# NF4 weights w1 and w2 quantised in the turned layout: block scales through memory in place of PE transposes

## What is computed

```
def nf4_quant_dequant(w):
    flat = w.reshape(-1, 64)
    absmax = max(abs(flat), axis=1, keepdims=True)
    normalized = flat / where(absmax == 0, 1.0, absmax)
    idx = searchsorted((NF4_CODE[:-1] + NF4_CODE[1:]) * 0.5, normalized)
    return (NF4_CODE[idx] * absmax).reshape(w.shape)
x = layernorm(x + layer1(x))
dq1, dq2, dq3 = (nf4_quant_dequant(w) for w in (w1, w2, w3))   # w1, w2: 1376 x 512, w3: 512 x 1376
h = silu(x @ dq1.T) * (x @ dq2.T)
out = layernorm(x + h @ dq3.T)
```

## Time and profile before

| | |
|---|---|
| median of 3 runs | 429.08 us (428.99 to 429.38) |
| the profiled execution | 429.23 us, its span 427.4 us |
| PE busy | 417.5 us, 98% |
| DVE, POOL, ACT busy | 307.1, 293.0, 265.2 us |
| PE transposes of w1 and w2 (L1258) | 88 instructions |
| moved by DMA | 26.51 MB |

### The profile page before, as it was taken

The page is one execution under the profiler, slowest core; times in us unless marked ns, Lnnn a source line. Parts: engine busy times, 40 slices in busy tenths (PEclk is TensorE's granted clock), DMA queues, the critical chain, the costliest instruction groups (busy, mean ns, idle before and its releaser), DMA issues.

```text
span 427.4 us, 5638 instructions
## 1 busy us (share of the span) xinstructions
PE 417.5 (98%) x1908; PEld 342.9 (80%) x1908; DVE 307.1 (72%) x379; ACT 265.2 (62%) x356; POOL 293.0 (69%) x230
## 2 busy tenths in 40 slices
PE   8999999999999999999999999999999999999992
PEld 6888888888878888888878888888888877888881
DVE  3639989979879966978358889978699974216025
ACT  5576776677668554638837797788677864332612
POOL 0079999888784698248943788899989993444330
PEclk9999999999999999999999999999999999999997
DMA  8994110000013442020060000000000000000202
GB/s 266 399 352 157 51 38 25 26 25 26 25 49 107 145 141 72 0 100 1 0 265 1 2 0 2 0 2 0 2 2 0 2 0 0 2 0 2 98 0 99
DMA packets 10876, 26.51 MB, mean 62 GB/s; under 512 B 1472, under 2 KB 1728, under 8 KB 10336
## 3 DMA queue, kind: packets, MB, share of 16 engines
q1 hardware_dynamic: 10848, 26.16, 17.8%
HBM read 24.06 MB, written 2.10 MB: 61 GB/s over the span
## 4 chain that ended last, share of the span: by engine, by line
PE 88%; ACT 3%; DVE 3%; issue 2%; POOL 2%; DMA 1%; SPq 0%; ACTq 0%; POOLq 0%
PE PS L1144 28%; PE PS L1145 28%; PE PS L1146 28%; PE PS L1258 2%; DMA h<-xT 1%; PE PS L1269 1%; ACT x_hi L557 1%; ACT l_hi L557 1%; POOL x_lo L1088 1%; POOL l_lo L1099 1%; DVE std L894 1%; DVE stats L875 0%; ACT R L643 0%; DVE R L870 0%; PE PS L1244 0%
## 5 line engine op out<-in xcount | busy, mean ns | idle before, releaser
L1069 POOL TENSOR_SCALAR level<-side 128x1024 f32<-128x1024 int8 (+2 forms) x119 | 133.0, 1118 | 13.7 <-ACT side L557 4.1
L1144 PE MATMUL PS<-x_hi,w_hi 128*128 128x512 f32 (+1 forms) x352 | 138.4, 393 | 0.3 <-DVE x_lo L944 0.3
L1146 PE MATMUL PS<-x_hi,w_lo 128*128 128x512 f32 (+1 forms) x352 | 137.2, 390 | 0.0
L1145 PE MATMUL PS<-x_lo,w_hi 128*128 128x512 f32 (+1 forms) x352 | 137.1, 390 | 0.0
L800 DVE TENSOR_TENSOR PS<-PS,level 128x1024 f32<-128x1024 f32 (+2 forms) x102 | 121.8, 1194 | 19.6 <-POOL level L1069 15.1
L557 ACT ACTIVATE side<-Q 128x1024 int8<-128x1024 f32 (+1 forms) x77 | 77.5, 1050 | 16.9 <-DVE PS L796 11.0
L1099 POOL TENSOR_TENSOR l_lo<-h,l_hi 128x512 fp32r<-128x512 f32 (+1 forms) x42 | 55.9, 1337 | 46.4 <-ACT l_hi L557 45.9
L1144 PEld LDWEIGHTS PS<-x_hi,w_hi 128*128 128x128 f32 (+1 forms) x352 | 65.2, 185 | 15.0 <-issue 0.7
L1146 PEld LDWEIGHTS PS<-x_hi,w_lo 128*128 128x128 f32 (+1 forms) x352 | 65.2, 185 | 14.8
L1145 PEld LDWEIGHTS PS<-x_lo,w_hi 128*128 128x128 f32 (+1 forms) x352 | 65.3, 185 | 14.2
L1144 PE MATMUL PS<-x_hi,l_hi 128*128 128x512 f32 x144 | 56.8, 394 | 0.6 <-POOL l_lo L1099 0.6
(11 more groups left out here) (77 smaller groups left out, 518.9 us busy)
## 6 DMA issues: line engine op xcount, KB each, us to landing
Q<-w SPq DMA_DIRECT2D x20, 256.0 KB, 9.8
raw<-w_in SPq DMA_DIRECT2D x9, 512.0 KB, 9.7
raw<-w_out SPq DMA_DIRECT2D x14, 256.0 KB, 2.6
raw<-w SPq DMA_DIRECT2D x2, 1376.0 KB, 7.8
R<-xN SPq DMA_DIRECT2D x2, 1024.0 KB, 5.1
out<-R SPq DMA_DIRECT2D x8, 256.0 KB, 2.0
raw<-w_fuse SPq DMA_DIRECT2D x7, 256.0 KB, 2.6
h<-xT SPq DMA_DIRECT2D x3, 512.0 KB, 6.9
```

The lines of the kernel that those rows point to most:

```text
L1069: g.tensor_scalar(level_of(s), side_of(s), LIMITS[k][1], LIMITS[k][0], ALU.min, ALU.max).then_inc(s_level, 1)
L1144: t_.matmul(dst, a_hi, b_hi, start=start, stop=False)
L1145: t_.matmul(dst, a_hi, b_lo, start=False, stop=False)
L1146: return t_.matmul(dst, a_lo, b_hi, start=False, stop=stop)
```

## The change

Units 1 to 10 are loaded already turned (`w12T`, an array that the host lays out so: partition = contraction index within a group of 128, then w1 or w2, group and row), and are quantised as they lie there. Only unit 0 is turned on PE. A block of 64 is then 64 partitions of one column, so the scales differ from column to column and are the same down 64 partitions. They are found as before from a second, natural copy (`w12`, rows laid out so that the blocks come in the order in which the turned unit needs them), then SP writes the block maxima and their reciprocals, 128 x 16 values each, to a scratch tensor in memory, and reads each back twice with a broadcast over 64 partitions, 4 KB per partition. POOL and DVE multiply by these wide tiles (L1213, L955). Unit 10 becomes 128 x 768 where it was 96 x 1024. The split of a turned chunk reads SBUF (`Q`) where it read PSUM.

There is no room of its own for the second copy and the wide scales. They stand in slots of `Q` that later units use, in the fifth raw slot (raw slots go from five to four, `W_AHEAD` from 4 to 3), and for unit 10 in `raw` and `l_hi`. The scales of a turned unit are now taken 12 steps ahead (unit 10: 7). SP gets a list of moves and a `SHARE` row of its own. On ACT, `split_x` of tiles 4 and 5 goes ahead of the scaling of tiles 6 and 7.

```diff
-SCALES_AHEAD, NORMALISE_AHEAD = 5, 3
+TURNED_AHEAD, LAST_AHEAD, SCALES_AHEAD, NORMALISE_AHEAD = 12, 7, 5, 3
+MOVES = [(1, "scales"), (2, "natural")]
+for u_ in range(1, C2):
+    MOVES.append((u_, "rcp"))
+    if u_ + 1 < C2:
+        MOVES.append((u_ + 1, "turned"))
+        if u_ + 2 == C2:
+            MOVES.append((u_ + 1, "natural"))
+        MOVES.append((u_ + 1, "scales"))
+        if u_ + 2 < C2 - 1:
+            MOVES.append((u_ + 2, "natural"))
+    MOVES.append((u_, "amax"))
+MOVES += [(C2 - 1, "w3 first"), (C2 - 1, "w3 second")]
-RAW_SLOTS = 5
-W_AHEAD = 4
+RAW_SLOTS = 4
+W_AHEAD = 3
 SHARE = {
+    "sync": [
+        0, 2, 1, 1, 5, 2, 3, 2, 5, 3, 4, 3, 2, 3, 0, 0, 0, 0, 0, 0, 0, 0, 0, 2, 0, 0, 0, 2, 0, 3, 0, 7, 0],
...
+            def to_memory(u):
+                n = unit_blocks(u)
+                sp.wait_ge(s_prep, scaled(u))
+                if u >= 3:
+                    sp.wait_ge(s_at, 32 * (u - 2))
+                for k, t in enumerate((amax, rcp)):
+                    sp.dma_start(scr[u % 2, k, 0:P * n].rearrange("(p n) -> p n", n=n), t[:, u % t.shape[1], 0:n]).then_inc(s_scr, 16)
+            def from_memory(u, k, to, done):
+                p = chunk_rows(u)
+                sp.wait_ge(s_scr, 32 * u)
+                n = 2 * DC * p
+                for r in range(2):
+                    sp.dma_start(to[r * BLOCK:(r + 1) * BLOCK, 0:n],
+                                 scr[u % 2, k:k + 1, r * n:(r + 1) * n].broadcast_to([BLOCK, n])).then_inc(done, 16)
+            def rcp_back(u):
+                if u >= 2:
+                    sp.wait_ge(s_nrm, normalised(u - 1))
...
+            def amax_back(u):
+                if u >= 2:
+                    sp.wait_ge(s_dq, quantised(u - 1))
+                if u == C2 - 1:
+                    sp.wait_ge(s_tile, TT)
+                from_memory(u, 0, amax_wide(u), s_at)
...
             def split_nf4(f):
                 beside()
-                act.wait_ge(s_tr, f + 1)
+                if f == 0:
+                    act.wait_ge(s_tr, 1)
+                else:
+                    act.wait_ge(s_dq, quantised(f))
                 wait_nf4_slot(act, f)
-                copy(in_slot(w_hi, f, 2 * DC * m).rearrange("p (c m) -> p c m", m=m),
-                     PS[:, NF4_BANK:NF4_BANK + 2, :].rearrange("p b (c m) -> p (b c) m", m=P)[:, :, 0:m]
-                     ).then_inc(s_whi4, 1)
+                copy(in_slot(w_hi, f, n), nf4_chunk(f)).then_inc(s_whi4, 1)
...
             def clamp_step(s):
-                for u in units_ahead(s, NORMALISE_AHEAD):
+                for u in normalise_due(s):
+                    if turned(u):
+                        pool.wait_ge(s_qT[u], 16)
+                        pool.wait_ge(s_rc, 32 * u)
+                        g.tensor_tensor(unit_read(u), unit_read(u), rcp_wide(u)[:, 0:unit_width(u)],
+                                        ALU.mult).then_inc(s_nrm, 1)
+                        continue
...
-                if x in (11, 13):
-                    transpose_nf4((x - 11) // 2)
+                if x == 11:
+                    transpose_first()
...
-                elif i == 2:
-                    transpose_nf4(2)
-                elif half == 1 and f + 2 < C2:
-                    transpose_nf4(f + 2)
```

More of the change, by code:

```diff
@@ L142, with steps_ahead, scales_due, normalise_due @@
 STEPS = [(u, k) for u in range(UNITS) for k in range(NB)]
-SCALES_AHEAD, NORMALISE_AHEAD = 5, 3
-def units_ahead(s, ahead):
-    return [u for u in range(UNITS) if max(0, NB * u - ahead) == s]
+TURNED_AHEAD, LAST_AHEAD, SCALES_AHEAD, NORMALISE_AHEAD = 12, 7, 5, 3
+def steps_ahead(u):
+    return SCALES_AHEAD if not turned(u) else TURNED_AHEAD if u < C2 - 1 else LAST_AHEAD
+def scales_due(s):
+    return [u for u in range(UNITS) if max(0, NB * u - steps_ahead(u)) == s]
+def normalise_due(s):
+    return [u for u in range(UNITS) if max(0, NB * u - NORMALISE_AHEAD) == s]
+MOVES = [(1, "scales"), (2, "natural")]
[10 more added lines that the diff above has]
+MOVES += [(C2 - 1, "w3 first"), (C2 - 1, "w3 second")]
 def adds(s):
@@ L243, in job_rows, with build @@
     return P if kind == "fuse" else rows(f, F1) if kind == "out" else rows(f, F2)
-def build(nc, xT, xN, w_pre, w_fuse, w_in, w_out, point, discount, w1, w2, w3, ident_in, out):
+def build(nc, xT, xN, w_pre, w_fuse, w_in, w_out, point, discount, w12, w12T, w3, ident_in, scr, out):
     with ExitStack() as ctx:
@@ L404, in wait_l_slot @@
                 wait_job_done(eng, n - L_SLOTS)
+            if n >= PASS_START[2]:
+                eng.wait_ge(s_dq, quantised(C2 - 1))
         def h_half(n):
@@ new lines, in load_natural, with move @@
+            def load_natural(u):
+                sp.wait_ge(s_prep, scaled(u - 1))
+                if u == C2 - 1:
+                    wait_split(sp, len(JOBS) - 1)
+                    wait_split(sp, VECTOR_LOW[-1])
+                load_unit(u)
+            def move(i):
+                u, what = MOVES[i]
+                if what == "scales":
+                    to_memory(u)
+                elif what == "rcp":
+                    rcp_back(u)
+                elif what == "natural":
+                    load_natural(u)
+                elif what == "amax":
+                    amax_back(u)
+                elif what == "turned":
+                    if u >= C2 - 2:
+                        sp.wait_ge(s_nrm, normalised(u - 1))
+                    load_turned(u)
+                elif what == "w3 first":
+                    sp.wait_ge(s_nrm, normalised(u))
+                    load_w3(0)
+                else:
+                    sp.wait_ge(s_dq, quantised(u - 1))
+                    load_w3(1)
@@ L512, in load_residual, with beside @@
+            turn, done = iter(SHARE["sync"]), [0]
+            def beside():
+                for _ in range(next(turn)):
+                    move(done[0])
+                    done[0] += 1
             def load_residual(a):
@@ L1352, in chunks_in, with blocks_of @@
         return np.ascontiguousarray(np.concatenate(parts, axis=1))
+    def blocks_of(*ws):
+        parts = [np.concatenate([w[0:P] for w in ws], axis=1)]
+        for u in range(1, C2):
+            m = chunk_rows(u)
+            both = np.stack([w[u * P:u * P + m].reshape(m, DC, 2, BLOCK) for w in ws])
+            parts.append(both.transpose(3, 0, 2, 1, 4).reshape(P, unit_blocks(u) * BLOCK))
+        return np.ascontiguousarray(np.concatenate(parts, axis=1))
     x = a(L0_attn_hidden_states)
@@ L1376 @@
     out = nc.dram_tensor("out", (TOK, D), F32, kind="ExternalOutput").ap()
-    build(nc, **args, out=out)
+    scr = nc.dram_tensor("scr", (2, 2, P * (UW // BLOCK)), F32, kind="Internal").ap()
+    build(nc, **args, scr=scr, out=out)
     r = run_bass_kernel_spmd(nc, [arrays], core_ids=[0])
```

104 lines of the change are left out of this document (67 added, 37 removed), and 18 rows, old and new, of the table SHARE.

## The result

The changed kernel takes **448.2 us** (median of 4 runs, 447.5 to 448.6) where the kernel before takes 429.2 beside it: a ratio of 1.0441, with a 95% interval of 1.0423 to 1.0459. It is 4.4% slower; the forecast was 424.1 us, and the range ended at 428.0.

The account below looks back on a forecast made before the run. PE was taken as the bound from its first product to its last. 429.23 - 8.5 (transposes) + 2.0 (end of the pairs) + 1.5 (second pass and layer's boundary) = 424.2, as a median 424.1 us; range 420.4 to 428.0.

Parts of the forecast that it names:

- Whatever leaves PE's list leaves the time.: Whole kernel: PE is the bound from first product to last, so removed work shortens the time if other engines deliver earlier.
- Removed from PE: 8.5: PE's list: ten of eleven groups of transposes go, 8.5 us, all on the path.
- Stage 1: Loop of scales through memory: 1 MB lands in 5.1 us against a 5.7 us gap, 7.0 us slack behind; cost nothing.
- The moved steps: Seven clamps and a normalise moved ahead of the pairs: POOL 7.7 and 2.0 us less there; about even at 216.37.
- End of the pairs: Before the w3 transposes: quantiser doesn't end early enough, 2.0 us of new wait for PE, bounds 0 and 4.6.
- the low part with two SBUF inputs: Chunks 2 to 10, in the pairs: each low part costs POOL 1.0 us, nine of them 9.3 us more.
- Layer's boundary: Unit 10's round trip delays tile 4's scaling, wanted at 229.2: 0 to 1.9 us of PE wait, 1.5 taken.
- the second pass: Around 216.37: PE arrives 0.87 us earlier, POOL has one clamp more but a normalise is gone; about even.
- Rival 2: Stage 1: read-back to 64 partitions runs at half rate, loop 7.6 us against 5.7; 426.6 us, chance 0.18.
- Its signs: Stage 1: 256 KB pieces from `scr` land in over 3 us, and POOL's normalise repeatedly waits 2 us for DMA.
- Rival 3: SP's queue in stage 1: round trip sets the quantiser's pace, landing 9.7 us, PE loses 13; 437 us, chance 0.08.

Follow-up runs that it names:

- e14: Kernel before the change with PE's transposes of chunks 1 to 10 left out and all else kept (products wrong): 431.1 us, ratio 1.004.
- e11: e1 with units 1 to 10 using their own 16 scales a row, no scales through memory, and low parts reading PSUM (computation changed): 429.4 us.
- e1: Changed kernel with the read-back of unit u+1's reciprocals put ahead of that of unit u's maxima in SP's list: 437.1 us.
- e6: e1 with the low parts of chunks 1 to 10 reading their first input from PSUM instead of SBUF (computation changed): 431.8 us.
- e15: e14 with the low parts reading the chunk in SBUF, as in the change: 438.1 us.
- e9: e1 with each half of w3 loaded in six pieces, the first unit's first, instead of one transfer: 434.8 us.
- e3: Changed kernel with the read-backs of units 2 to 9 left out, stores and arithmetic kept: 436.2 us.
- e12: e9 with the engines' steps about 10 us later near 133 and 173 us, and SP's list moved with them: 440.6 us.

## Why the prediction was wrong

**"Whatever leaves PE's list leaves the time."** This first sentence failed. It has the condition with it, "as long as the other engines deliver earlier by the same amount", and I had seen that the quantiser arrives 0.06 us ahead of need in one place and 0.63 late in another. e14 shows what that is worth where the quantiser isn't made earlier: nothing of the 8.5 us. A busy share of 98% and a chain of 88% PE don't say that PE is the only bound; in e14 the loop of ACT, POOL and DVE is as long, and in the kernel before it was hidden under PE. e11 shows the other side: where the quantiser has a lead, the 7.6 us of the pairs do leave the time.

**Removed from PE: 8.5.** Right as a price in the list, as e11's pairs show. It isn't a gain.

**Stage 1: "I cost stage 1 at nothing".** This is the step that failed most, and 11.1 of the 19 us hang on it (e1): 5.2 in the pairs of layer 1, and the rest behind them, since the low parts of the next stage come late too. I had set 5.1 us, the landing of 1 MB alone, against a gap of 5.7. Measured from the first of the four issues to the normalise it is 6.7 to 7.3 us, once 8.3. Left out were the issues themselves, the slower landing of pieces with 64 partitions, and the turned copy of the next unit, which SP issues right behind, so that 1.5 MB share the engines. I also left out 0.5 us on each normalise: the row of 1.91 is one with a narrow operand, and I counted the wide operand only for unit 10. All go into the same loop, once a unit.

**The moved steps.** The seven clamps and the normalise that go ahead of the pairs were credited with 9.7 us of POOL at the pairs' end, and priced only with 1.0 us at 216.37, "about even". There was no term for the first pass, where the low parts come just in time. With the work of the engines as before, that pass still costs e11 6.8 us, its longest wait 2.60 us; e14, with the steps where they were, loses nothing there. That it is the steps and not another part of the layout (the second copies' loads, for one) is the nearest reading; no run moves the steps alone.

**End of the pairs: took 2.0, bounds 0 to 4.6.** In the changed kernel PE idles 3.9 us from 290 to 390, which looks like a term inside its bounds. Counted by the start of the same products, though, the pairs give back 1.6 of 7.6 us, so 6.0 are lost; in e1 it is 5.2, and with the low parts from PSUM, in e6, 0.4. The term that was too small is the low part with two SBUF inputs. It was priced at 1.0 us of POOL (and, as an estimate by the Trainium skill, "SBUF — State Buffer", section "Who interferes with whom", at 1.2). POOL's busy time moves by 7.1 us for ten of them, 0.7 each, so both are too high, and the row's is the nearer. But DVE itself pays 0.55 us for each as well, which had no price, and since both engines sit in one loop, e6 gives 5.3 us and e15 - e14 7.0.

**Layer's boundary: took 1.5 for the second pass and the boundary.** The size is right, the place only in part. PE waits 1.37 us at 237.08, but this is the wait of 0.63 that stood at 216.37, for the same low part of POOL, and not one for tile 4's scaling. Where that one was expected, behind the first pair of layer 2, PE starts the next product 0.6 us later.

**Rival 2, pieces with 64 partitions: right in stage 1, wrong as a whole.** Its signs both came: the pieces land in 4.0 and 4.8 us in the median, and waits of 1.1 to 3.2 us recur. It gave 9.5 us of slip for the last w_in low part and 2.5 of PE; measured are 10.5, with the longer normalise in it, and a wait of 2.25. It stopped there, though: the low parts behind this one had no slack left either, and 15.6 us more are lost in the next pass. And the cure was the order and not the rate: e1 keeps the pieces and loses nothing in the pairs of layer 1.

**Rival 3: 437 us, chance 0.08.** It had the place of the cause, SP's queue in stage 1, and came nearest with its number, but partly by luck. A landing of 9.7 us and 13 us of idle time in stage 1 are nowhere: PE idles 3.0 us between 90 and 120. The chance rested on "memory is nearly idle then", which is true of the kernel before and beside the point: the reciprocals were issued late. Its number was too low as well, because it had neither the pass behind nor the lowered clock, 9.9 us in which the same products took longer.

**Not priced at all:** the load of w3 behind unit 10 (2.3 us, e9).

What is left open: e11 equals the kernel before and e14 is 1.7 us above it, but they lose their time in different places. e11 is 7.8 us late before the pairs of layer 2 and loses nothing in them; e14 isn't late before them and loses all. I haven't found an order that has both halves and turns PE's 8.5 us into time, nor shown that there is none. No version is clearly faster than the kernel before; the best whole one of the changed layout is e9, 434.8 us, with two edits: the order in SP's list and the pieces of w3.

## What to carry to other kernels

When an engine at 98% is fed just in time by a loop of others, removing its work may buy nothing until the loop is shorter; before the real change is written, leave the work out (e14: a few lines) and time that. When steps are moved, price them where they land too, and compare the start of the same product in both traces: it shows the stretch in which the time goes, which idle time alone does not (6.0 us are lost in the pairs of layer 2, and PE idles only 4.1 from 240 to 380). Where a queue carries loads behind waits, write down for each issue the event that frees its target and the event that the queue waits for in front of it: where the two differ by a unit of work, swap them (e1: one line, 11 us). And a wait of 2 us or more on TensorE can cost more than its length, for the clock behind it: 9.9 us more for 9.3 of such waits in the changed kernel, 2.5 more for 4.3 in e14.

## What the runs showed of the hardware

- Behind most of PE's waits of 2 to 5 us the granted clock of a window of 10 us falls, to between 0.66 (e14, 350 to 360) and 0.89. Behind four of them it stays at 1.00: 2.56 us in e9 and 2.53 in e6, both near 136, 3.10 in e3 at 176.35 and 2.16 in e12 at 173.78. In the changed kernel waits of 0.63, 1.12 and 0.66 us between 326 and 361 left it at 1.00. What the lower clock costs is PE's busy time above the 417.5 - 8.5 = 409.0 us of the kernel before without transposes: 9.9 us in the changed kernel, 5.2 in e1, 3.9 in e9, 2.5 in e14.
- A transfer whose source has an outermost dimension of 2 arrived at 51 GB/s with 0.14 of the engines' time, and SP's next issue took 7.80 us where it takes 0.59 in the changed kernel: the queue holds up its issuer.
- Pieces of 256 KB that go to 64 partitions land some 1.1 us apart with all 16 engines busy, 0.6 of the best rate in a slice.
- Instructions of DVE and POOL that both read SBUF hold each other up: 1.77 for 1.21 us on DVE in the mean, 1.21 where POOL is idle beside it, and 0.7 us each on POOL. A DVE instruction of 16 elements a row, 0.17 us by itself in e1, lasts up to the end of the POOL normalise of 2.40 us beside it; the mean is 0.97 us, where it was 0.45 in the kernel before.
- The stores of 8 KB, 64 bytes a partition, land in 2.2 us in the median; the pieces that read them back, 256 KB each, in 4.0 and 4.8.
